# Block 0's first transfers, idle matmuls during its waits, and a new order of tile kinds

## The reference

```
e = stack([tbl_f[ids[:, f]] for f in range(39)], axis=1)        # 1024 x 39 x 16
x0 = xk = e
for l in range(3):
    z = relu(einsum('bhd,bkd,hks->bsd', x0, xk, W_l) + b_l)      # W_l: 39 x K x 128
    if l < 2:
        xk = z[:, :64]; direct.append(z[:, 64:])
    else:
        direct.append(z)
z = sum(concatenate(direct, axis=1), axis=-1)                    # 1024 x 256
y = relu(relu([z, dense] @ W_top1 + b) @ W_top2 + b) @ W_top3
```

## Time and profile before

| what | value |
|---|---|
| median of 3 runs | 1244.64 us (1243.7 to 1245.4) |
| profiled execution, its time | 1244.94 us |
| its span | 1243.1 us |
| instructions | 14868 |
| PE busy | 1179.9 us, 95% |
| POOL busy | 1002.6 us, 81% |
| DVE busy | 1061.9 us, 85% |
| ACT busy | 580.7 us, 47% |

### The profile page before, as it was taken

One profiled execution on the slowest core, in us unless ns is written; L12 is line 12 of the kernel. 1 busy time (PEld: TensorE's weight loads), 2 busy tenths in 40 slices (PEclk: granted clock), 3 DMA queues, 4 the chain that ended last, 5 costly groups with the idle time before them and its releaser, 6 DMA issues.

```text
span 1243.1 us, 14868 instructions
## 1 busy us (share of the span) xinstructions
PE 1179.9 (95%) x3856; PEld 726.5 (58%) x3856; DVE 1061.9 (85%) x927; ACT 580.7 (47%) x563; POOL 1002.6 (81%) x629
## 2 busy tenths in 40 slices
PE   0289999999999999999999999999999999999999
PEld 0155666656565665656566565656656565666665
DVE  2278998989899898989889898998989898998984
ACT  1145444444545444454544445454444545444545
POOL 6678897998889899888989888888988889765651
PEclk9999999999999999999999999999999999999999
DMA  4785726365472626556262745637274563627000
GB/s 125 242 256 191 223 63 218 125 182 201 157 226 60 218 108 206 177 172 211 84 204 97 225 159 172 211 102 215 79 233 140 172 211 123 212 72 231 9 1 1
DMA packets 110269, 196.21 MB, mean 158 GB/s; under 512 B 52975, under 2 KB 64334, under 8 KB 110249
## 3 DMA queue, kind: packets, MB, share of 16 engines
q1 hardware_dynamic: 100009, 193.33, 47.2%
q0 software_dynamic: 10240, 2.64, 2.0%
HBM read 193.36 MB, written 12.78 MB: 166 GB/s over the span
## 4 chain that ended last, share of the span: by engine, by line
PE 69%; POOL 13%; DVE 8%; issue 6%; ACT 2%; DMA 2%; POOLq 0%; SPq 0%; DVEq 0%; ACTq 0%
PE acc L845 67%; POOL lo L464 7%; POOL emb L454 6%; DVE prod L706 3%; DVE lo L719 2%; ACT hi L556 2%; DVE acc L706 1%; DVE hi L716 1%; DMA x_tiles<-x_rows 0%; DMA x_rows<-x_rows 0%; DVE xk L706 0%; PE acc L925 0%; POOLq L163 0%; DMA x_rows<-emb 0%; ACT xk L522 0%
## 5 line engine op out<-in xcount | busy, mean ns | idle before, releaser
L706 DVE TENSOR_TENSOR prod<-x_tiles,xk 128x1024 f32<-128x1024 f32 (+2 forms) x643 | 757.5, 1215 | 123.9 <-PE acc L845 83.4
L464 POOL TENSOR_TENSOR lo<-prod,hi 128x1024 fp32r<-128x1024 f32 (+1 forms) x288 | 690.5, 2400 | 141.1 <-ACT hi L556 136.4
L845 PE MATMUL acc<-prod,wfull 128*128 128x512 f32 (+2 forms) x1408 | 660.6, 593 | 0.0
L556 ACT ACTIVATE hi<-prod 128x1024 fp32r<-128x1024 f32 (+1 forms) x291 | 308.4, 1060 | 406.3 <-DVE prod L706 322.4
L845 PE MATMUL acc<-hi,whi 128*128 128x512 f32 (+1 forms) x800 | 353.0, 441 | 57.7 <-ACT hi L556 57.6
L845 PEld LDWEIGHTS acc<-prod,wfull 128*128 128x128 f32 (+2 forms) x1408 | 266.8, 189 | 205.7 <-issue 177.4
L454 POOL DMA_INDIRECT emb<-table,block_idx x320 | 308.6, 964 | 69.3 <-issue 63.9
L845 PE MATMUL acc<-lo,whi 128*128 128x512 f32 (+1 forms) x736 | 316.1, 517 | 2.4 <-POOL lo L464 1.2
L845 PE MATMUL acc<-hi,wlo 128*128 128x512 f32 (+1 forms) x800 | 316.1, 395 | 0.0
L845 PEld LDWEIGHTS acc<-hi,whi 128*128 128x128 f32 (+1 forms) x800 | 150.9, 189 | 112.4 <-issue 72.2
L845 PEld LDWEIGHTS acc<-lo,whi 128*128 128x128 f32 (+1 forms) x736 | 138.3, 190 | 133.2 <-issue 104.0
(11 more groups left out here) (72 smaller groups left out, 163.4 us busy)
## 6 DMA issues: line engine op xcount, KB each, us to landing
x_tiles<-x_rows SPq DMA_DIRECT2D x304, 512.0 KB, 5.1
x_rows<-x_rows SPq DMA_DIRECT2D x16, 624.0 KB
x_tiles<-x_rows SPq DMA_DIRECT2D x32, 256.0 KB, 5.6
x_stack<-x_rows SPq DMA_DIRECT2D x48, 156.0 KB
emb<-table,block_idx POOLq DMA_INDIRECT x320, 3.8
x_rows<-emb SPq DMA_DIRECT2D x16, 152.0 KB, 3.3
x_tiles<-w SPq DMA_DIRECT2D x1, 768.0 KB, 6.1
x_tiles<-w SPq DMA_DIRECT2D x1, 704.0 KB, 8.6
```

The lines of the kernel that those rows point to most:

```text
L464: nc.gpsimd.tensor_tensor(lo[0:r, product_slot(j), :], prod[0:r, product_slot(j), :], hi[0:r, part_slot(j), :].bitcast(f32), ALU.subtract) ...
L556: nc.scalar.activation(hi[0:r, part_slot(j), :], held(n, parity, j)[0:r, :], ACT.Copy).then_inc(hi_ready, 1)
L706: nc.vector.tensor_tensor(held(n, parity, j)[0:r, :], in0, in1, ALU.mult).then_inc(product_ready, 1)
L845: mm = nc.tensor.matmul(z[:, c], w[0:r], part[0:r, c], start=first and i == 0, stop=last and i == len(weights) - 1)
```

## The change

In words:

- The kinds of layer 0 go from GFFGFFF to FGFFGFF, and those of layer 1 start with FGDGF in place of GFDGF. So the G tiles of layer 0 are its tiles 1 and 4 (they were 0 and 3), and the first G of layer 1 is tile 1 (it was tile 0). The number of tiles of each kind is the same.
- Block 0's indices and bases are loaded by two transfers of their own (SP and ACT issue one each), added by POOL in the first 20 columns alone, and gathered from at once; the add for all blocks comes behind block 0's gathers.
- Block 0's embeddings are written a second time, to a DRAM tensor x0_head that has 41 rows (the first two are there again at the end); its stack is loaded from there, by ACT's queue, and no longer from the repeated rows by SP's. SP's tile loads still wait for the repeated rows.
- DVE makes `wlo` of layers 1 and 2 only when block 0's rows have been written.
- PE runs 24 matmuls of 512 columns on weights once the rows have been written, then the prologue, then 10 more; nobody reads their results.
- One transfer of weights is split in two, since the tile that is skipped is no longer the first.

The core of the diff:

```diff
-KINDS = ["GFFGFFF", "GFDGF" * 2 + "GFHGF" + "GFDGF", "GFFGF" + "GFFGD" + "GFHGF" + "GFDGF"]
+KINDS = ["FGFFGFF", "FGDGF" + "GFDGF" + "GFHGF" + "GFDGF", "GFFGF" + "GFFGD" + "GFHGF" + "GFDGF"]
...
+    x0_head = nc.dram_tensor("x0_head", [FIELDS + 2, COLS], f32, kind="Internal").ap()
...
+            sp.dma_start(block_idx[0][:, :], ids[:, 0:PAIRS]).then_inc(first_ids_loaded, 16)
             sp.dma_start(rows_idx[:, :], ids).then_inc(ids_loaded, 16)
             sp.dma_start(base_sb[:, :], base).then_inc(ids_loaded, 16)
             load_weights()
+            def write_head():
+                row = lambda r, dims: bass.AP(x0_head.tensor, r * COLS, dims)
+                sp.dma_start(row(0, [[DIM, 128], [2 * COLS, PAIRS - 1], [1, DIM]]),
+                             emb[0][:, 0:(PAIRS - 1) * DIM].rearrange("p (i d) -> p i d", d=DIM)
+                             ).then_inc(head_written, 16)
+                sp.dma_start(row(FIELDS - 1, [[DIM, BLOCK], [1, DIM]]),
+                             emb[0][0:BLOCK, (PAIRS - 1) * DIM:PAIRS * DIM]).then_inc(head_written, 16)
+                sp.dma_start(row(FIELDS, [[DIM, 128], [1, DIM]]), emb[0][:, 0:DIM]).then_inc(head_written, 16)
+
             write_rows(0, 0)
+            write_head()
             repeat_rows(0)
-            load_stack(0)
+            sp.wait_ge(rows_repeated, 16)
...
+            pool.wait_ge(first_ids_loaded, 32)
+            nc.gpsimd.tensor_tensor(block_idx[0][:, :], block_idx[0][:, :], first_base[:, :], ALU.add
+                                    ).then_inc(idx_ready, 1)
+            pool.wait_ge(idx_ready, 1)
+            gather(0, 0, PAIRS)
             pool.wait_ge(ids_loaded, 32)
             nc.gpsimd.tensor_tensor(rows_idx[:, :], rows_idx[:, :], base_sb[:, :], ALU.add).then_inc(idx_added, 1)
             pool.wait_ge(idx_added, 1)
-            take_indices(0, 0, reuse=False)
-            gather(0, 0, PAIRS)
             take_indices(1, 1, reuse=False)
             gather(1, 0, 12)
...
+            act.dma_start(first_base[:, :], base[:, 0:PAIRS]).then_inc(first_ids_loaded, 16)
...
             act.wait_ge(bias_loaded, 48)
+            act.wait_ge(head_written, 3 * 16)
+            for g in range(PER):
+                act.dma_start(x0_stack[g * FIELDS:(g + 1) * FIELDS, :], x0_head[g:g + FIELDS, :]).then_inc(stack_loaded, 16)
             copy_stack(PROLOGUE)
...
             for l in range(3):
                 dve.wait_ge(whi_ready, l + 1)
+                if l == 1:
+                    dve.wait_ge(rows_written, 32)
...
+            def warm_up(passes):
+                at = SPLIT_AT[1]
+                for i in range(passes):
+                    nc.tensor.matmul(accumulator(0, 0)[:, 0:BANK], whi[:, at + i % 4, :],
+                                     whi[:, at:at + BANK // LAYER, :].rearrange("p w s -> p (w s)"), start=True, stop=True)
+
             pe.wait_ge(wlo_ready, 1)
+            pe.wait_ge(whi_ready, 3)
+            pe.wait_ge(rows_written, 32)
+            warm_up(24)
             contract(PROLOGUE, L0, L2, accumulator(0, 1))
+            warm_up(10)
             pe.wait_ge(wlo_ready, 3)
```

More of the change, by code:

```diff
@@ L71 @@
 FULLS = [[t for t, k in enumerate(ks) if k == "F"] for ks in KINDS]
+SQUARE = (SPLITS[0] + FULLS[0]).index(0)
 SPLIT_AT = [0, len(SPLITS[0]), len(SPLITS[0]) + len(SPLITS[1])]
@@ L174, in build @@
         base_sb = sb("base_sb", [128, BLOCKS * PAIRS], i32)
+        first_base = sb("first_base", [128, PAIRS], i32)
         block_idx = [sb(f"block_idx{p}", [128, PAIRS], i32) for p in range(2)]
@@ L226, in build @@
         y_sb = x0_tiles[0:1, own + 3, :]
+        first_ids_loaded = sem("first_ids_loaded")
+        head_written = sem("head_written")
         ids_loaded = sem("ids_loaded")
@@ L311, in load_weights @@
                 sp.dma_start(w0f_stage[0:LAST0, len(FULLS[0]) - 1, :], w0[0:LAST0, T0 - 1, :]).then_inc(w0_loaded, 16)
-                sp.dma_start(w0t_stage[0:ROWS0, 1:T0 - 1, :], w0t[:, 1:T0 - 1, :]).then_inc(w0_loaded, 16)
+                sp.dma_start(w0t_stage[0:ROWS0, 0:SQUARE, :], w0t[:, 0:SQUARE, :]).then_inc(w0_loaded, 16)
+                sp.dma_start(w0t_stage[0:ROWS0, SQUARE + 1:T0 - 1, :], w0t[:, SQUARE + 1:T0 - 1, :]).then_inc(w0_loaded, 16)
                 sp.dma_start(w0t_stage[0:LAST0, T0 - 1, :], w0t[0:LAST0, T0 - 1, :]).then_inc(w0_loaded, 16)
                 sp.wait_ge(w0_cleared, 1)
-                sp.dma_start(w0t_stage[FIELDS:ROWS0, 0, :], w0t[FIELDS:ROWS0, 0, :]).then_inc(w0_loaded, 16)
+                sp.dma_start(w0t_stage[FIELDS:ROWS0, SQUARE, :], w0t[FIELDS:ROWS0, SQUARE, :]).then_inc(w0_loaded, 16)
                 for l, b in enumerate((b0, b1, b2)):
@@ L446, in take_indices @@
                 pool.wait_ge(idx_ready, m + 1)
+                if is_step(m, 2):
+                    pool.wait_ge(head_written, 3 * 16)
                 if reuse:
@@ L670, in _ @@
         def _(dve):
-            nc.vector.memset(w0t_stage[:, 0, :], 0.0).then_inc(w0_cleared, 1)
+            nc.vector.memset(w0t_stage[:, SQUARE, :], 0.0).then_inc(w0_cleared, 1)
             nc.vector.memset(direct2[:, :], 0.0).then_inc(direct2_cleared, 1)
             dve.wait_ge(direct2_cleared, 1)
-            dve.wait_ge(w0_loaded, 6 * 16)
+            dve.wait_ge(w0_loaded, 7 * 16)
             n, f = len(SPLITS[0]), len(FULLS[0])
```

## The result

The changed kernel takes 1250.4 us (median of 6 runs, 1249.71 to 1251.25), the kernel before 1245.23 us beside it (6 runs). The ratio is 1.0043, with a 95% interval of 1.003 to 1.0056: slower by some 5 us. The forecast was 1253.3, with a range of 1247 to 1258 and 87% for slower.

The account below looks back on a forecast made before the run. The bound was a closed loop of PE (95% busy), ACT and POOL, 71.87 us a round. A 15.5 us loss less 6.8 gained gave +8.7 on 1244.94, forecast as 1253.3 us, range 1247 to 1258 (8 in 10).

Parts of the forecast that it names:

- The round: Layer 0's second G: its hi runs behind the direct relu, delaying POOL and PE 1.11 us in 14 rounds, 15.5 us lost.
- Layer 1: First G moved to tile 1: POOL starts as before, since ACT's slot wait covers the later product; no cost.
- The start: The chain to the first product, the prologue and step 0's layer 1 gain 6.8 us in all, bounds 3.5 to 8.3.
- indices: Start: small transfers and a 20-column add let the first gather begin at about 4.7, gaining 1.5 us (0.3 to 1.9).
- gathers: Start: block 0's gathers no longer overlap DVE's long wlo subtractions, gaining 1.9 us (1.3 to 2.0).
- transfers: Start: SP no longer issues or queues three stack loads ahead of the first tile, gaining 1.7 us (0 to 2.4).
- prologue: PE's layer 0 before the steps ends 15.6 us after the first product, not 16.0: 0.5 us gained (0 to 1.0).
- step 0's layer 1: With a warm PE clock and F first, first product to ACT's relus takes 32.8 us, not 34.0: 1.2 us gained.
- the round doesn't grow: Rival, 10%: POOL's run ends in time or PE's wait at tile 10 is eaten; only the start changes, 1237.8 us.
- the start doesn't gain: Rival, 12%: table load, shared transfer engines and a fallen clock cut the start's gain to 3.2 us, giving 1256.9 us.
- POOL starts later still: Rival, 4%: layer 1's first G comes a full product later, adding 0.8 us a round, 11 us more, 1264 us.
- the loss is only half a microsecond a round: Rival, 4%: a smaller loss in each round about cancels the start's gain, giving 1243 to 1247 us.

Follow-up runs that it names:

- e3: The kernel before, with only ACT's direct relu moved ahead of the hi of layer 0's tile 3: 1258.64 us, ratio 1.0115.
- e1: The changed kernel with ACT's direct relu moved behind the hi of layer 0's tile 4: 1246.5 us, ratio 1.0017 to the kernel before.
- e2: The changed kernel with the old kinds of layer 0 (GFFGFFF), all else new: 1236.97 us, ratio 0.9942 to the kernel before.
- e4: The kernel before with the new kinds alone and the weight transfer split that they need: 1255.24 us, ratio 1.009.
- e11: The changed kernel with block 0's indices made the old way (one add over 320 columns, a copy, then gathers): 1253.73 us, ratio 1.0076.
- e10: The kernel before with layer 2's gathers spread behind its first 6 subtractions and not 4, nothing else: 1239.19 us, ratio 0.9953.
- e5: The changed kernel without both groups of idle matmuls (24 and 10): 1250.61 us, ratio 1.0043 to the kernel before.
- e9: The changed kernel with DVE making wlo of layers 1 and 2 without waiting for the written rows: 1252.75 us, ratio 1.0069.

## Why the prediction was right, point by point

**The round.** The main step held in place and in kind: the second G's hi came behind the direct relu, POOL's run began that much later, and PE waited at tile 10. e3 shows it alone, in the kernel before. The size was set a little too high: 1.11 us a round, 15.5 in all. It was 1.00 from relu to `lo` and 0.95 in the pitch, about 13.3 us in all (12.3 in the 13 intervals and 1.0 in step 0). I had let the hi start when the relu had ended, but ACT starts a hi 1.01 us behind the start of that relu (679.91 to 680.92), before its 1.11 us are over.

**The second limit.** I worked out that POOL would be free 0.4 us ahead of the new `lo`'s start. It was free 0.28 ahead by its idle time, and e1 gained just that in the pitch. So the loss was not ACT's order alone. Had the relu alone been mended, most of the loss would have stayed, since the first G tile had moved too.

**Layer 1.** Nothing was taken for its new kinds, because ACT's slot and not the product sets the first hi. e2 has them and a pitch of 71.80.

**The start.** Forecast 6.8 us, found about 7.8 in the two profiled executions; e2, which has the new start without the prologue's 0.5, is 7.4 us below its kernel before by the medians. The split is that of one pair of executions, and their starts vary by 2 us (e4):

| term | forecast | by the traces | how |
|---|---|---|---|
| indices | 1.5 | 3.0 | first gather 6.23 to 3.27 |
| gathers | 1.9 | 1.5 | first to twentieth gather 25.86 to 24.32 |
| transfers | 1.7 | 2.1 | first row write to first product 15.86 to 13.75 |
| prologue | 0.5 | 0.5 | first product to step 0's first product 18.60 to 18.14 |
| step 0's layer 1 | 1.2 | 0.7 | first product to relus 34.04 to 33.29 |

The term that was mis-sized most is the indices. The two small transfers had both landed by 2.76, when the add starts, where I let it start at about 3.7; and the gather followed the add by 0.28 us of idle, where I kept the 0.90 of the earlier trace rows, which had stood behind a copy. e11 shows the 0.90 again, with the copy. Of the gathers' 1.9 us, 0.4 did not come: one of the twenty, at 8.41, took 1.39 us.

The transfers' 2.1 is in part luck of the pair. In the kept traces with the old stack load and no head (before, e3, e4, e10) the first row write is 14.64 to 15.89 us ahead of the first product, 15.3 on average; in the nine with the new one it is 13.56 to 15.68, 14.3 on average. So the gain is about 1.0 us and not the forecast 1.7, and it has a part that I had put at nothing. I took the three head writes to fit into SP's wait for the rows. They did not: the repeat was issued 4.65 us behind the first row write and not 3.85 (34.67 - 30.02 against 38.42 - 34.57), about 0.8 us lost in every trace with the head. Against it stands that from the repeat's issue to the first tile's it is 4.70 us and not 6.03, 1.3 gained. The rest, from the tile's issue to the first product, spreads too widely to say: 4.72 to 6.01 us before and 4.18 to 6.16 after. The Trainium skill's rule on queues ("DMA: Bandwidth & Descriptors", Issuing engines are not separate DMA queues) would have had 1.2 for this term, issue time alone. The traces agree with it: 1.3 in SP's issuing, and no gain in the transfers themselves that stands out of the spread.

The prologue's gain is right, though I had put PE's end at 66.4 where its last record ends at 66.70.

For step 0's layer 1 I had credited the warm clock with about 0.7. e5 shows that with F first it is worth nothing there, and so is the first group, whose clock had fallen by the time it was wanted. The Trainium skill ("TensorE: Matmul & The Clock Gate", What's actually happening) is right that the clock falls when PE idles, and the trace agrees (0.59 from 45 to 49); but with F first the time of this layer did not hang on it.

**The sum.** 13.3 - 7.8 = 5.5 us, and the spans differ by 1248.5 - 1243.1 = 5.4. The forecast's 8.7 was 2.2 too high on the loss and 1.0 too low on the gain. That the gain was off by no more is partly luck: the indices were 1.5 too low while the gathers and step 0's layer 1 together were 0.9 too high.

**The rivals.** That the round doesn't grow is refuted by the pitch, that the start doesn't gain by the first wait at 125.81, that POOL starts later still by a pitch below the forecast's 73.0, and that the loss is only half a microsecond a round by its 0.95.

## What to carry to other kernels

When PE is 95% busy and another engine 80%, look for the closed loop between them and ask what moves on it. Here a change of which tile is split put one product and one relu onto it, each of about a microsecond. They delay the same run of work side by side, so only the later one counts: 0.95 us, fourteen times over, which took back more than a shorter start had gained once. Test the order of an engine that is half idle by one constant (e3) before trusting that it has room. And where other work, as the gathers here, stands in front of the result that PE waits for, move some of it behind that result: by one constant this gained 5 us in each of the two kernels with the old kinds, more than the new stack load and the idle matmuls together.

## What the runs showed of the hardware that I had not expected

- An ACT activation that reads SBUF started 1.01 us behind the start of one that reads PSUM and takes 1.11 us, in the changed kernel and in e3, which have this order (679.91 to 680.92, 686.25 to 687.26).
- A recorded wait of PE was shorter than what the pitches give for it, by 0.3 to 0.5 us: 0.18 for 0.46, 0.93 for 1.41. The profile models the ends of matmuls, which may be why; that is not shown.
- PE's granted clock was 0.59 from 45 to 49, after PE had stood still for 3.0 us (42.06 to 45.05), and it stayed high (1.00 from 59 to 66) over the 1.3 us between the ten idle matmuls and step 0's first (recorded wait 1.32 us).
- The start of one and the same code differed by 2.2 us between executions (step 0's first product at 66.87 in e3 and 69.03 before). 1.2 of it lies between the first row write and the first product (14.64 and 15.86), 0.7 in the twenty gathers (25.20 and 25.86).
- POOL's gathers of 0.94 us took 1.24 to 2.22 us beside DVE's long subtractions, in the old place (e9: 1.24 and 1.62) and in the new one (after, beside block 1's gathers: 1.46 and 1.62).
